# Full attention of a hybrid network: query and key parts made on chip in f32r for tiles of 32 rows, instead of bf16 parts brought through DRAM for 72 rows

## The reference

```
qkv = x @ W_qkv + b_qkv (+ x @ A @ B * 2 in the first)      # 2 x 1024 x 384
attn = softmax(q @ k.T * 8 ** -0.5)        # per batch and head, 1024 x 1024
        # second attention: scores above the diagonal are -1e9
out = (attn @ v) @ W_proj + b_proj
x = x + out                                # of layernorm(x)
```

## Time and profile before

| | us |
|---|---|
| median of 3 runs | 6326.32 (6325.24 to 6332.52) |
| profiled execution, its own time | 6325.83 |
| its span, first to last instruction | 6324.0 |
| TensorE busy | 5607.0 (89%) |
| VectorE busy | 4380.8 (69%) |
| ScalarE busy | 4012.0 (63%) |
| GpSimd busy | 2640.0 (42%) |
| mean granted TensorE clock | 0.94 |

### The profile page before, as it was taken

The page is one execution under the profiler, slowest core; times in us unless marked ns, Lnnn a source line. Parts: engine busy times, 40 slices in busy tenths (PEclk is TensorE's granted clock), DMA queues, the critical chain, the costliest instruction groups (busy, mean ns, idle before and its releaser), DMA issues. The chain is left out here.

```text
span 6324.0 us, 156761 instructions
## 1 busy us (share of the span) xinstructions
PE 5607.0 (89%) x57236; PEld 3888.6 (61%) x57236; DVE 4380.8 (69%) x6822; ACT 4012.0 (63%) x7609; POOL 2640.0 (42%) x2385
## 2 busy tenths in 40 slices
PE   6996776689999999999998699699999999999997
PEld 2222333167777777777776222387777777777775
DVE  6884555377777777777775588577777777677774
ACT  3663444267777777777675266577777767677774
POOL 2001000055655555555554200265555555555552
PEclk7997887689999999999999699899999999999998
DMA  1001000000000000000000100000000000000000
GB/s 50 24 18 38 25 23 7 14 20 18 16 22 17 20 16 21 17 18 21 18 18 15 39 24 23 26 17 15 22 17 18 21 17 20 15 22 17 18 21 17
DMA packets 182018, 130.28 MB, mean 21 GB/s; under 512 B 82941, under 2 KB 170137, under 8 KB 177817
## 3 DMA queue, kind: packets, MB, share of 16 engines
q1 hardware_dynamic: 181272, 120.40, 6.9%
HBM read 96.89 MB, written 10.49 MB: 17 GB/s over the span
## 5 line engine op out<-in xcount | busy, mean ns | idle before, releaser
L1651 POOL TENSOR_TENSOR cross<-raw,tab_b 128x512 f32<-128x512 f32 x768 | 989.4, 1313 | 311.2 <-ACT raw L1521 309.4
L731 DVE TENSOR_REDUCE arena<-PS 128x1 f32<-128x512 f32 (+2 forms) x1408 | 858.7, 650 | 374.9 <-PE PS L540 233.6
L697 ACT ACTIVATE arena<-PS 128x1024 f32<-128x1024 f32 (+1 forms) x704 | 677.9, 967 | 505.1 <-PE PS L560 337.9
L1657 POOL CAST kT_b<-kT 128x512 bf16<-128x512 f32 x384 | 273.3, 712 | 1287.1 <-ACT kT L1575 1287.1
L1744 DVE TENSOR_TENSOR oT<-PS,rec_den 128x288 f32<-128x288 f32 (+1 forms) x768 | 326.5, 425 | 637.5 <-ACT rec_den L1555 637.4
L540 PE MATMUL PS<-arena 72*128 72x512 bf16 (+2 forms) x1408 | 554.3, 397 | 217.1 <-DMA arena<-parts_k 157.1
L1715 DVE TENSOR_TENSOR rot<-PS,tab_a 128x512 f32<-128x512 f32 x768 | 523.3, 686 | 287.5 <-PE PS L1400 153.9
L1521 ACT COPY raw<-PS 128x512 f32<-128x512 f32 x768 | 449.1, 590 | 342.5 <-PE PS L1400 302.4
L1369 PE MATMUL PS<-qT,kT 64*128 64x96 f32 x8448 | 659.2, 286 | 0.0
L1547 ACT ACTIVATE PT<-PS 128x576 f32<-128x576 f32 (+1 forms) x768 | 469.0, 611 | 253.2 <-PE PS L1369 241.6
L1731 DVE TENSOR_TENSOR rot<-rot,cross 128x1024 f32<-128x1024 f32 x384 | 611.2, 1592 | 8.5 <-POOL cross L1651 8.2
(11 more groups left out here) (242 smaller groups left out, 12729.6 us busy)
## 6 DMA issues: line engine op xcount, KB each, us to landing
w_qk<-in_w_pairs SPq DMA_DIRECT2D x196, 128.0 KB, 2.1
arena<-parts_q SPq DMA_DIRECT2D x72, 192.0 KB
arena<-parts_k SPq DMA_DIRECT2D x72, 192.0 KB
w_v<-in_w_pairs SPq DMA_DIRECT2D x100, 128.0 KB, 2.2
w_o<-in_w_out_pairs SPq DMA_DIRECT2D x192, 64.0 KB, 1.8
xs<-x_tok SPq DMA_DIRECT2D x24, 256.0 KB
xs<-x_tok SPq DMA_DIRECT2D x24, 254.0 KB
parts_q<-arena SPq DMA_DIRECT2D x18, 256.0 KB
```

The lines of the kernel that those rows point to most:

```text
L697: nc.scalar.activation(PT[n % 4].rearrange("p (a n) -> p a n", a=2)[:, :, first_q:512], PS[:, 2 * (n % 2):2 * (n % 2) + 2, first_q:512], A ...
L731: nc.vector.tensor_reduce(maxima[:, hh, qt, kh:kh + 1], bank[:, 0:keys_of(qt, kh)], AX.X, ALU.max).then_inc(mx_red, 1)
L1651: nc.gpsimd.tensor_tensor(dst[:, :, :, o:o + 32], src[:, :, :, other:other + 32], tab[:, :, o:o + 32].unsqueeze(2).broadcast_to([128, 8, 2 ...
```

## The change

All three full attentions are rewritten inside their opening and main part. What the diff does:

- The weights of q and k are spread by DVE copies, so that one projection of 128x512 (`piece`) yields, for one group and one half of the tokens, each head's 8 channels three times, in its own 32 rows. ACT reads that bank twice (rounded to f32r, and whole, each with a sign per row), and the difference of the two is the operand: two parts, three products, 24 rows and a row for the maximum. A group needs four pieces. POOL subtracts them, DVE for group 0.
- The pieces of a later group are projected inside the main part. Nothing of q and k goes through DRAM; the four small row transfers of a half stay. Of these, the maximum has one f32r row where two bf16 rows were.
- Maxima and scores are issued in pairs, one head in rows 32i to 32i+31, the next in the 32 below, into two banks.
- Maxima, pieces, V projections, turned maxima and turned outputs share a ring of three banks (4, 5, 7), in one list `order` made by `couples_at` and `late`. A bank is filled again when what was in it three places before has been taken.
- Value matmuls are cut into two halves of the queries, one after each score pair, where the step is wide enough.
- The number of maxima ahead of the first score is 40 in the lora and plain attentions, 44 in the causal one. All groups are written out, without a loop.
- The workspace is sized by stage; two constants are loaded beside the weights; x + b_proj is one POOL instruction, before 16.

```diff
-        QS = [cut(2 * N, after_xt if m == 0 else None).bitcast(BF16).rearrange("p (h n) -> p h n", h=4) for m in range(2)]
...
-        full_qk = {n: cut(B * N) for n in "qk"}
...
-        parts = {n: cut(3 * B * N // 2).bitcast(BF16).rearrange("p (i n) -> p i n", i=3) for n in "qk"}
...
+        whole = [cut(512) for _ in range(2)]
...
+        high = [rounded(f"high{m}", [128, 512]) for m in range(2)]
+        operand = {n: [rounded(f"{n}_parts{m}", [128, N]) for m in range(3)] for n in "qk"}
...
+        LEAD = 3 if causal else 2
+        AHEAD = 2 * (STEPS - second + LEAD)
+        START = -AHEAD // 2
...
+        def piece_step(g, f):
+            return g * STEPS + START - 6 + f
+        def late(t, slot):
+            names = []
+            if slot == 0:
+                names += [("piece", g, f) for g in range(1, HGROUPS) for f in range(4) if piece_step(g, f) == t]
+                names += [("rows", half) for half in range(2 * HGROUPS) if found_in(half) + 1 == t]
+            else:
+                names += [("V", k) for k, at in enumerate((-3, -2, 2 * STEPS + 4, 2 * STEPS + 8)) if at == t]
+                names += [("out", half) for half in range(2 * HGROUPS) if last_step(half) + 3 == t]
+            return names
+        RING = (4, 5, 7)
...
             def _(sp):
-                def load(i, par):
-
-                    for a in range(3):
-                        sp.dma_start(QS[par][24 * a:24 * a + 24, :, :],
-                                     scratch_qk["q"][bass.ds(i, 1), a, :, :].broadcast_to([3, HD, 4 * N])).then_inc(loaded, 16)
-                        sp.dma_start(KS[par][24 * a:24 * a + 24, :, :],
-                                     scratch_qk["k"][bass.ds(i, 1), :, :, :].rearrange("o c d n -> (o c d) n")).then_inc(loaded, 16)
...
-                def store(name, part, b, stored):
...
+                for half in range(2 * HGROUPS):
+                    i, hf = half // 2, half % 2
+                    taken(sp, "rows", half)
                     for hh in range(4):
+                        dst = operand["q"][i % 3][32 * hh:32 * hh + 1, 512 * hf:512 * hf + 512].bitcast(F32)
+                        sp.dma_start(dst, max_rows[half % 2][4 * hh:4 * hh + 4, :].bitcast(F32)).then_inc(rows_in, 16)
...
             def _(pool):
+                def low_part(g, f):
+                    n, half = PIECES[f]
+                    taken(pool, "piece", g, f)
+                    need(pool, st_full, (g - 2) * 2 * STEPS)
+                    nc.gpsimd.tensor_tensor(operand[n][g % 3][:, 512 * half:512 * half + 512], whole[f % 2], high[f % 2][:, :], ALU.subtract).then_inc(made, 1)
...
             def _(pe):
...
+                def bank_for(*name):
+                    n = number[name]
+                    need(pe, free[n % 3], n // 3)
+                    return PS[:, RING[n % 3], :]
+                def piece(g, f):
+                    n, half = PIECES[f]
+                    bank = bank_for("piece", g, f)
+                    nc.tensor.matmul(bank, spread[n][:, g % 4, :], tokens(2 * (g // 4) + half), start=True, stop=True).then_inc(full, 1)
...
+                def maximum(g, couple):
...
+                    banks = [bank_for("max", g, couple, h) for h in range(2)]
+                    for h in range(2):
+                        r = slice(32 * (2 * m + h), 32 * (2 * m + h) + 32)
+                        last = nc.tensor.matmul(banks[h][:, 0:keys], q[r, 128 * qt:128 * qt + 128], k[r, 512 * kh:512 * kh + keys],
+                                                start=True, stop=not masked, tile_position=(32 * (2 * m + h), 0), skip_group_check=True)
...
+                for t in range(START, ALL + 3):
+                    for slot, (g, couple) in enumerate(couples_at(t)):
+                        if couple:
+                            maximum(g, couple)
+                        if 0 <= t < ALL:
+                            scores(2 * t + slot)
+                        fills(t, slot)
+                        if 0 < t <= ALL:
+                            values(t - 1, slot)
...
             def _(act):
...
+                def evacuate(g, f):
...
+                    bank, bank_free = filled(act, "piece", g, f)
+                    s = 2 * (n == "k")
+                    nc.scalar.activation(high[f % 2][:, :], bank, ACT.Identity, scale=signs[:, s:s + 1], bias=b_high[:, c:c + 1])
+                    nc.scalar.activation(whole[f % 2], bank, ACT.Identity, scale=signs[:, s + 1:s + 2], bias=b_whole[:, c:c + 1]).then_inc(bank_free, 1)
```

More of the change, by code:

```diff
@@ new lines, in fills @@
+                def fills(t, slot):
+                    for name in late(t, slot):
+                        if name[0] == "piece":
+                            piece(name[1], name[2])
+                            continue
+                        if name[0] == "rows":
+                            pe.wait_ge(m_ready, name[1] + 1)
+                            last = nc.tensor.matmul(bank_for(*name)[0:16, 0:128], neg_max[name[1] % 2], ident_b[:, :], start=True, stop=True)
+                        elif name[0] == "V":
+                            bank = bank_for(*name)
+                            for j in range(4):
+                                last = nc.tensor.matmul(bank[:, 128 * j:128 * j + 128], tokens(name[1])[:, 128 * j:128 * j + 128], w_qkv[:, 256:384], start=True, stop=True)
+                        else:
+                            pe.wait_ge(o_ev, name[1] + 1)
+                            bank = bank_for(*name)
+                            for j in range(4):
+                                last = nc.tensor.transpose(bank[:, 128 * j:128 * j + 128], OT[name[1] % 2][:, 128 * j:128 * j + 128], ident[:, :])
+                        last.then_inc(full, 1)
@@ new lines, in _ @@
+                for t in range(START, ALL + 3):
+                    for half in range(2 * HGROUPS):
+                        if last_step(half) + 2 == t:
+                            out_half(half)
+                    if 0 <= t < ALL:
+                        exponentials(2 * t)
+                    for name in late(t, 0):
+                        if name[0] == "rows":
+                            rows(name[1])
+                        else:
+                            evacuate(name[1], name[2])
+                    if 0 <= t < ALL:
+                        exponentials(2 * t + 1)
```

567 lines of the change are left out of this document (239 added, 328 removed).

## The result

The changed kernel takes 6290.22 us (median of 4 runs, 6281.19 to 6304.42), the kernel before 6329.42 us beside it (4 runs, 6325.24 to 6334.12): ratio 0.994, 95% interval 0.9919 to 0.9961. So it is 39 us faster where 214 were forecast, and outside the forecast's range. The profiled execution is the slowest of its four (6304.42, span 6302.5); the mean granted clock of TensorE fell from 0.94 to 0.92.

The account below looks back on a forecast made before the run. TensorE and DVE take turns, neither full. Savings of 2 x (31.5 + 37.5) + 20 + 56 = 214 us from 6325.83 gave 6112 us; range 5985 to 6235, with 6020 to 6195 given 0.52.

Parts of the forecast that it names:

- if the clock stays up: Causal main part: 41.5 us a group against 49.5 provided the clock doesn't fall; seven groups save 56 us.
- The clock's rival: All three attentions: side-by-side pairs stream too little, TensorE falls to 1.2 GHz, 584 us if all ran low; chance 0.10.
- Masked slots, 1.5 us with switches of 0.12: Causal main part: a half step with masks takes 1.5 us, including five tiling changes of 0.12 us each; 16 a group.
- Openings, 2 x 31.5: Stretch up to the first exponential in both unmasked attentions: 31.5 us saved in each.
- The causal opening: Stretch up to the causal attention's first exponential: 20 us saved, with 44 reductions ahead and masks at the low clock.
- Unmasked main parts, 2 x 37.5: Both unmasked attentions after their first exponential: 48 us a group against 52.1, 3.0 a step, 37.5 us saved each.
- the unhidden rest of a slot: Unmasked main parts: 0.05 us per half step between reductions that DVE can't cover, giving 2.57 us a step.
- The extras: Unmasked main parts: pieces, turned maxima and outputs, waits and negations add 9.0 us a group before any overlap.
- in series: Unmasked main parts: a group without overlap takes 16 x 2.57 + 9.0 = 50.1 us.
- Handing over costs what it gave: Rival: main parts stay as now, three banks for pairs holding hardly more than two for singles; 6230 us, chance 0.19.
- DVE alone: Rival: a group's additional work vanishes into the other engine's waits and DVE sets the time; 5990 us, chance 0.16.
- The wait of 9.74 us: Causal main part: TensorE's 9.74 us wait for the next group's loads goes, tiling switches eating part of the gain.

Follow-up runs that it names:

- the run with filling and all masks: Changed kernel with all masks kept, plus matmuls adding bf16 zeros onto bank 6 ahead of the values in the causal attention's narrow steps: 6243.78 us, 0.9861.
- the run without masks: Changed kernel with all masks of the causal attention left out, for maxima and scores, so masking isn't computed: 6190.59 us, 0.9761.
- the split pair: Changed kernel; in the unmasked attentions the second maximum of a pair is issued behind the two scores, each waiting for its own bank: 6267.47 us, 0.9885.

## Why the prediction was wrong, step by step

- **The step that failed is the causal main part's condition "if the clock stays up".** Its price was right: 41.5 us a group was forecast, 43.1 measured where the clock was held (the run with filling and all masks). But in the changed kernel's causal main part 2.4 GHz held nowhere for longer than 17 us. Groups of 55 to 66 us made +101 of the forecast -56. These 157 us are four fifths of the 192 that the profiled execution missed (22 us faster than the trace before, where 214 were forecast); by the medians the miss is 175. That the clock makes the loss is shown by one group's instructions at either clock. Why it falls is shown in part: filling in the narrow steps cut the time at 1.2 GHz from 430 to 270 us, and what makes the rest of the falls is open.
- **The clock's rival named the right cost and place, and the argument against it was wrong.** It had the price nearly right (1.6 us more a step at the low clock; all at 1.2 GHz a group took 66.4, which is 1.9 a step above 43.1) and named the causal attention as the emptier one (54% of streaming). Its reason, too little streaming by the pairs, isn't borne out: widening or doubling them didn't bring the clock back. It was dismissed because TensorE would be busy throughout and the clock had then risen, by six us with nothing but full-width work. The trace shows 122.73 of 123 us busy at 1.2 GHz: here the records' busy time doesn't tell whether the clock will return. Also, the chance was given for all three attentions at once; each stage had to be judged by itself. The two unmasked ones ran at 1.00.
- **Masked slots, 1.5 us with switches of 0.12**: from a pair in row tiles to the masks 0.23 is lost at 2.4 GHz and 0.3 at 1.2, twice or more what rows 8 showed for another direction, though 0.10 and 0.16 of it go without a switch too; back to row tiles 0.10 to 0.11. At full clock the group came out near the forecast all the same; at the low clock TensorE is the bound and all of it counts.
- **Openings, 2 x 31.5**: 29 and about 30 (16, and 14 that the stages ahead of the plain attention took more: its first projection stands 2522.7 us behind the causal one's last copy before, 2537.1 now). Right. First reduction 32.74 against 34.2, first exponential 68.36 against 65.8: from one to the other 35.6 us in place of 31.6, since at the low clock a pair comes every 1.63 us, where two reductions of 0.70 were put. The causal opening gave 13.5 of 20; in the run without masks the same stretch was 103.1 us instead of 106.2, so masks account for 3, and the rest isn't split up.
- **Unmasked main parts, 2 x 37.5**: 21 and 20. Row tiles run side by side as forecast, and DVE's reductions took 0.65 as before. The mis-sized term is the unhidden rest of a slot: not 0.05 but 0.10, since a pair waits for two of three banks; split, the slot is 1.23, and nothing is left of it. That makes a step 2.68, not 2.57, and a group 1.8 us longer, nearly all that lies between the 48 forecast and the 50.0 measured. The extras came as taken, 7.2 against the 6.9 that 48 implies. That 50.0 is also the 50.1 "in series" is chance: it has cheaper steps and dearer extras.
- **"Handing over costs what it gave"** (0.19) would have meant 52 us a group: it is 50.0, so about half of the forecast gain was lost to it. DVE alone (45.6) was not reached; with the split pair it is 47.4.
- The wait of 9.74 us is gone, as forecast. But in the kernel before, TensorE came out of it into dense work, and the clock, low from 830.5, was back at 840.7; in the changed kernel it fell in the narrow steps and then stayed down for 100 us and more.

The Trainium skill (TensorE: Matmul & The Clock Gate, A second HAM failure mode: psum-queue depth-cycling) tells of a kernel in which short idle times between groups of matmuls, with PSUM banks cycled through, make the clock swing between its two levels. The causal attention agrees with this: waits of 0.2 us ahead of each fall, and one rise a group at most. The same page of the Trainium skill (Part 1: The HAM clock gate) has activity release the throttle. Read by the records' busy share, that would have happened between 622 and 745 (122.73 of 123 us busy), and it didn't; the measurement decides.

## What to carry to other kernels

Judge the clock stage by stage, and by the emptiest steps of a stage, not by its busy share: making matmuls cheaper where they are narrow can turn TensorE from idle at 2.4 GHz into the bound at 1.2. Filling put only into the empty steps, in the tiling that is already set and ahead of a wait, made the attention 39 us shorter; streaming added in every step made it 16 and 86 us longer. Which of the three (place, tiling, position ahead of the wait) matters wasn't tried one by one. And with a ring of banks, let each matmul wait for its own bank even where two are meant to run side by side: it gave 17 us an attention where the clock held. But in all four runs with it one of the two unmasked attentions at least had 36 to 81 us at 1.2 GHz, in place of 8 to 14 in the changed kernel, so look at the clock again afterwards.

## What the runs showed of the hardware beyond that

- From a pair in 32-row tiles to masks on the full array 0.23 us are lost at 2.4 GHz and 0.3 at 1.2; back 0.10 to 0.11; from row tiles to 32-column tiles 0.14. Between two pairs in row tiles, without a switch, 0.10 and 0.16 are lost.
- The same instructions of one causal group took 43.1 us at 2.4 GHz and 70.1 at 1.2.
- When the clock rises is partly chance: four executions of the run with filling and all masks took 6215.70 to 6280.46 us, the shorter the higher their mean granted clock (0.939 to 0.927).
- The untouched layers took 14 us more between the causal and the plain attention and 21 less behind the latter than in the kernel before. Part of it goes with the clock: the first six window layers had 87 us at 1.2 GHz in place of 68, the second six 60 in place of 90. Why it differs no run tested; it stays open.
